# Attention of a two-layer block: batch 0 projected in two groups of four tiles, with the loads of K and Q between them

## The reference

```
q, k, v = xn @ Wq.T + bq, xn @ Wk.T + bk, xn @ Wv.T + bv
li, lj  = xn @ rel_W[:, :d].T, xn @ rel_W[:, d:].T
probs   = softmax(li[:, :, None, :] + lj[:, None, :, :] + rel_b, -1)     # three ways
bias    = einsum('bijk,hk->bhij', probs, logical_bias)
gate    = sigmoid(xn @ gate_W.T + gate_b)
weights = softmax(q k^T / 4 + gate * bias, -1)
x       = x + (weights @ v) @ Wo.T + bo
```

## Time and profile before

| | us |
|---|---|
| median of 3 runs | 6366.53 (6357.88 to 6370.67) |
| profiled execution, span | 6366.2 |
| first weight instruction of DVE | 26.96 |
| first score matmul of PE | 208.43 |
| first score row of DVE | 211.97 |
| last output store of the attention issued | 3194.31 |

### The profile page before, as it was taken

One profiled execution on the slowest core, in us unless ns is written; L12 is line 12 of the kernel. 1 busy time (PEld: TensorE's weight loads), 2 busy tenths in 40 slices (PEclk: granted clock), 3 DMA queues, 4 the chain that ended last, 5 costly groups with the idle time before them and its releaser, 6 DMA issues. The chain is left out here.

```text
span 6366.2 us, 126141 instructions
## 1 busy us (share of the span) xinstructions
PE 5502.0 (86%) x40354; PEld 3579.2 (56%) x40354; DVE 4670.8 (73%) x6108; ACT 4439.8 (70%) x7115; POOL 3699.2 (58%) x2063
## 2 busy tenths in 40 slices
PE   3688888888888888888879977999999979999999
PEld 3466666666666666665534434555555546666665
DVE  1688988888888888888878958999999961221221
ACT  1698998989899898999936668888888851111111
POOL 2677777777777777777610008999999960000000
PEclk7899999999999999999989989999999999999999
DMA  1212111121211212120035556555555541111110
GB/s 34 43 27 46 29 37 35 27 47 26 47 27 28 45 26 48 28 45 18 13 120 189 213 187 217 204 186 206 189 199 202 206 164 34 33 33 49 33 33 10
DMA packets 470082, 538.37 MB, mean 85 GB/s; under 512 B 251056, under 2 KB 345008, under 8 KB 469568
## 3 DMA queue, kind: packets, MB, share of 16 engines
q1 hardware_dynamic: 469568, 531.63, 27.3%
HBM read 370.18 MB, written 161.35 MB: 83 GB/s over the span
## 5 line engine op out<-in xcount | busy, mean ns | idle before, releaser
L317 DVE CUSTOM_DVE_ANT_0 srow<-srow,ps_s,cur 128x1024 f32<-128x1024 f32 x1024 | 1304.0, 1273 | 262.9 <-PE ps_s L465 180.8
L394 ACT ACTIVATE srow<-srow,nmax 128x1024 f32<-128x1024 f32 x1024 | 1190.9, 1163 | 207.6 <-DVE nmax L317 195.0
L403 ACT COPY AT<-ps_t 128x512 f32<-128x512 f32 x2048 | 1104.9, 597 | 74.8 <-PE ps_t L476 74.0
L476 PEld LDWEIGHTS ps_t<-ident,srow 128*128 128x128 f32 x8192 | 962.7, 143 | 279.1 <-ACT AT L403 84.1
L476 PE MATMUL ps_t<-ident,srow 128*128 128x128 f32 x8192 | 1105.0, 279 | 13.1 <-ACT AT L403 8.7
L1725 POOL TENSOR_TENSOR c_hc<-c_hs,c_cs 128x1024 f32<-128x1024 f32 x432 | 1009.8, 2363 | 60.8 <-DVE c_hs L1827 58.9
L465 PE MATMUL ps_s<-K,Q 96*128 96x512 bf16 x2048 | 632.3, 391 | 440.3 <-DVE nmax L317 318.5
L306 DVE SCALAR_TENSOR_TENSOR srow<-ps_p,rho,R 128x1024 f32<-128x1024 f32 x768 | 975.4, 1270 | 13.7 <-ACT ps_p L357 9.2
L1686 PE MATMUL c_ps_y<-c_hc,c_ident 128*128 128x512 f32 x2048 | 944.8, 594 | 30.0 <-POOL c_hc L1725 17.1
L1827 DVE TENSOR_TENSOR_SCAN c_hs<-c_da,c_pd 128x1024 f32<-128x1024 f32 x384 | 860.2, 2274 | 54.6 <-PE c_pd L1677 54.0
L1770 ACT ACTIVATE c_sT<-c_dxT,c_bT 128x256 f32<-128x256 f32 x1536 | 668.4, 494 | 106.8 <-PE c_pd L1677 96.6
(11 more groups left out here) (196 smaller groups left out, 8361.8 us busy)
## 6 DMA issues: line engine op xcount, KB each, us to landing
c_cs<-bc_d SPq DMA_DIRECT2D x256, 512.0 KB, 4.3
c_bs<-bc_d SPq DMA_DIRECT2D x64, 512.0 KB, 6.7
parts_d<-parts SPq DMA_DIRECT2D x65, 384.0 KB, 3.3
K<-parts_d SPq DMA_DIRECT2D x192, 128.0 KB, 4.6
Q<-parts_d SPq DMA_DIRECT2D x384, 64.0 KB, 2.9
sz_d<-b_sz SPq DMA_DIRECT2D x16, 1024.0 KB, 7.1
xv_d<-b_xv SPq DMA_DIRECT2D x16, 1024.0 KB, 7.7
dt_d<-b_ab SPq DMA_DIRECT2D x16, 1024.0 KB, 4.2
```

Of the source, the lines that this page charges most:

```text
L317: nc.vector.tensor_tensor_reduce(r[:], r[:], ps_s[:], cur[k][:, h:h + 1], BIG, ALU.add, ALU.min, nmax[:, h % NROW:h % NROW + 1]).then_inc( ...
L394: nc.scalar.activation(r[:], r[:], ACT.Exp, scale=-1.0, bias=nmax[:, h % NROW:h % NROW + 1]).then_inc(e_ok, 1)
L403: nc.scalar.copy(AT[h % NAT][:, HG * half:HG * half + HG, :], ps_t[:, half]).then_inc(at_ok, 1)
L476: last = nc.tensor.transpose(ps_t[:, half, i, :], rows_sb[h % NROW][:, j * P:(j + 1) * P], ident[:])
```

## The change

- SP no longer loads `b_gT` and `lbT`. DVE makes them from the row of biases with a mask (a reduction of the identity) and three more reductions. The waits for weights now ask for six DMAs.
- The `project` loop is gone. The eight tiles of batch 0 are two groups `g` of four: one x load of 512 KB, statistics and normalisation of four tiles, eight transposes into `ps_t`, matmuls with 512 columns where there were 128 (`pe_g_d`, `pe_g_g`, `pe_g_q`, `pe_g_k`) into `ps_p`, `ps_s`, `ps_t`, V in pairs of tiles through `ps_s` (`pe_g_v`). DVE takes the remainder and the low part, which POOL took. Buffers of the loop that are still unused hold the group's data.
- Parts are stored by four DMAs of 384 KB a group. Behind group 0's, SP loads Q6 of tile 0 and the first 512 tokens of K6 (24 DMAs of 64 KB without waits, `g_k6`), behind group 1's the other 512 tokens, by head groups with the waits of before.
- Tile 0's three-way softmax has all its POOL passes on DVE, in between group 1's.
- Tile 8 is projected in between: turned and D and gate behind group 0's, Q and K behind group 1's V.
- The semaphores that the loop counts get their start values by increments; the next stage clears all of the attention's semaphores on SP.
- The loop over tiles, its order and its instructions are the same.

The diff, cut to the lists and to one helper of each kind:

```diff
+        def sp_first_keys(sp, half):
+            cut = slice(4 * P * half, 4 * P * half + 4 * P)
+            for g in range(HG):
+                if half:
+                    alone(sp, k6_in, 96 * g, sp_own)
+                for s, part in enumerate(K_PART):
+                    sp.dma_start(K6[HD * s:HD * s + HD, HG * g:HG * g + HG, cut],
...
+        def dve_g_rem(dve, g, s):
+            dve.wait_ge(g_hi, 2 * g + s + 1)
+            nc.vector.tensor_tensor(GQK[g][s], GQK[g][s], GPARTS[:, 2 * g + s, 0], ALU.subtract).then_inc(g_rem, 1)
+        def pe_g_rows(dst, w, g, m):
+            for c in range(DC):
+                last = nc.tensor.matmul(dst, w[:, c], GXT[g][:, c, :], start=(c == 0), stop=(c == DC - 1))
...
             def start(sp):
-                sp_keys(sp, 0)
+                for s in range(2):
+                    sp_g_parts(sp, 0, s)
+                alone(sp, g_st, 64, sp_own)
                 sp_q6(sp, 0, 0)
+                sp_first_keys(sp, 0)
+                for s in range(2):
+                    sp_g_parts(sp, 1, s)
+                alone(sp, g_st, 128, sp_own)
+                sp_first_keys(sp, 1)
                 sp_parts(sp, NT)
...
             def start(pool):
-                front(pool, NT)
-                pool_rel(pool, 0, 0, 0)
...
+                pool_g_rstd(pool, 0)
+                pool_rstd(pool, NT)
+                pool_g_rstd(pool, 1)
+                pool_gT(pool, NT)
+                pool_rem(pool, NT)
+                pool_lo(pool, NT)
                 pool_f(pool, 0, 0, 1)
...
             def start(dve):
+                dve_g_qk(dve, 0)
+                for s in range(2):
+                    dve_g_rem(dve, 0, s)
+                for s in range(2):
+                    dve_g_lo(dve, 0, s)
+                for j in range(2):
+                    dve_g_v(dve, 0, j)
+                dve_g_gate(dve, 0)
+                dve.wait_ge(g_dc, 2)
                 for step in range(2):
                     dve_rel(dve, 0, 0, step)
+                for n in range(2):
+                    first_rel(dve, n)
+                dve_g_qk(dve, 1)
+                dve_g_rem(dve, 1, 0)
+                first_sum(dve, 0)
+                dve_g_rem(dve, 1, 1)
+                first_sum(dve, 1)
+                for s in range(2):
+                    dve_g_lo(dve, 1, s)
+                for j in range(2):
+                    dve_g_v(dve, 1, j)
+                first_t(dve)
                 dve_y(dve, 0)
+                first_p(dve, 1)
+                first_p(dve, 0)
+                dve_qk(dve, NT)
+                dve_g_gate(dve, 1)
                 dve_f(dve, 0, 0, 0)
...
+            def start(pe):
+                pe_g_t(pe, 0)
+                pe_xT(pe, NT, 0)
+                pe.wait_ge(w_ready, 1)
+                pe_g_d(pe, 0)
+                pe_g_g(pe, 0)
+                pe_d(pe, NT, 0)
                 pe_g(pe)
+                pe.wait_ge(w_ready, 2)
+                pe_g_q(pe, 0)
+                pe_g_k(pe, 0)
+                pe_g_t(pe, 1)
+                for j in range(2):
+                    pe_g_v(pe, 0, j)
+                pe_g_d(pe, 1)
+                pe_g_g(pe, 1)
+                pe_g_q(pe, 1)
+                pe_g_k(pe, 1)
+                for j in range(2):
+                    pe_g_v(pe, 1, j)
                 for half in range(2):
+                    pe_qk_proj(pe, NT, 0, half)
+                pe.wait_ge(g_k6, 16 * 24)
...
                 pe_s(pe, 0, 0, 0)
...
+            for used in HELD["done"]:
+                sp.sem_clear(used)
```

More of the change, by code:

```diff
@@ new lines, in act_g_t, with act_g_d, act_g_e @@
+        def act_g_t(act, g):
+            act.wait_ge(g_t, g + 1)
+            nc.scalar.copy(GXT[g], ps_t[:].rearrange("p c i t -> p c (i t)")).then_inc(g_tc, 1)
+        def act_g_d(act, g):
+            act.wait_ge(g_d, g + 1)
+            nc.scalar.copy(Dj[:, :, 4 * P * g:4 * P * g + 4 * P], wide(ps_p)).then_inc(g_dc, 1)
+        def act_g_e(act, g):
+            act.wait_ge(g_g, g + 1)
+            for m in range(DC):
+                last = nc.scalar.activation(GE[g][:, m, :], ps_s[:, 4 * P * m:4 * P * m + 4 * P], ACT.Exp, scale=-1.0,
+                                            bias=b_gT[:, m:m + 1])
+            last.then_inc(g_ec, 1)
@@ new lines, in pe_g_t @@
+        def pe_g_t(pe, g):
+            pe.wait_ge(g_xn, g + 1)
+            if g:
+                pe.wait_ge(g_qc, g)
+            for c in range(DC):
+                for i in range(4):
+                    last = nc.tensor.transpose(ps_t[:, c, i, :], GXN[g][:, i, c * P:(c + 1) * P], ident[:])
+            last.then_inc(g_t, 1)
+        def pe_g_rows(dst, w, g, m):
+            for c in range(DC):
+                last = nc.tensor.matmul(dst, w[:, c], GXT[g][:, c, :], start=(c == 0), stop=(c == DC - 1))
+            return last
@@ new lines, in pe_g_d, with pe_g_g @@
+        def pe_g_d(pe, g):
+            pe.wait_ge(g_tc, g + 1)
+            if g:
+                pe.wait_ge(g_kc, g)
+            for i in range(2):
+                last = pe_g_rows(ps_p[:, 4 * P * i:4 * P * i + 4 * P], w_dj[:, :, i, :], g, i)
+            last.then_inc(g_d, 1)
+        def pe_g_g(pe, g):
+            if g:
+                pe.wait_ge(g_vc, 2 * g)
+            for m in range(DC):
+                last = pe_g_rows(ps_s[:, 4 * P * m:4 * P * m + 4 * P], w_gr[:, :, m * P:(m + 1) * P], g, m)
+            last.then_inc(g_g, 1)
@@ new lines, in pe_g_q, with pe_g_k, pe_g_v @@
+        def pe_g_q(pe, g):
+            for m in range(DC):
+                last = pe_g_rows(ps_t[:, m].rearrange("p i t -> p (i t)"), w_qk[:, :, m * P:(m + 1) * P], g, m)
+            last.then_inc(g_q, 1)
+        def pe_g_k(pe, g):
+            pe.wait_ge(g_dc, g + 1)
+            for m in range(DC):
+                last = pe_g_rows(ps_p[:, 4 * P * m:4 * P * m + 4 * P], w_qk[:, :, D + m * P:D + (m + 1) * P], g, m)
+            last.then_inc(g_k, 1)
+        def pe_g_v(pe, g, j):
+            if j == 0:
+                pe.wait_ge(g_ec, g + 1)
+            else:
+                pe.wait_ge(g_vc, 2 * g + 1)
+            for i in range(2):
+                at = (2 * j + i) * P
+                for c in range(DC):
+                    last = nc.tensor.matmul(ps_s[:, 4 * P * i:4 * P * i + D + H + 2], GXT[g][:, c, at:at + P],
+                                            w_vg[:, c, 0:D + H + 2], start=(c == 0), stop=(c == DC - 1))
+            last.then_inc(g_v, 1)
@@ L559, in followed, with run @@
             return t > 0 and t <= (B - 1) * NT if isinstance(t, int) else pro
[L561 removed]
+        def run(eng, start, body, finish, ends=False):
             def pairs(first, start_i, par, b):
@@ L645, in _ @@
-            sp.sem_inc(parts_w, 16)
-            sp_x(sp, 0, 0)
-            run(sp, start, project, body, finish, ends=True)
+            sp.sem_inc(parts_w, 16 * NT + 16)
+            sp.sem_inc(x_in_s, 16 * NT)
+            for g in range(2):
+                sp.dma_start(GX[g], x_in[4 * P * g:4 * P * g + 4 * P, :].rearrange("(i p) d -> p i d", p=P)
+                             ).then_inc(g_in[g], 16)
+                loads = (((row[:], rows.partition_broadcast(P)), (ident[:], ident_in),
+                          (w_vg[:], wvg[:, 0:D + H + 6].rearrange("(c p) n -> p c n", p=P)), (b_qk[:], bqk)),
+                         ((w_qk[:], wqk.rearrange("(c p) n -> p c n", p=P)),
+                          (w_o[:], wvg[:, D + H + 6:].rearrange("(c p) n -> p c n", p=P))))[g]
+                for dst, src in loads:
+                    sp.dma_start(dst, src).then_inc(w_in, 16)
```

290 lines of the change are left out of this document (191 added, 99 removed).

## The result

The changed kernel takes 6224.6 us (median of 4 runs, 6220.4 to 6226.2) against 6366.5 for the kernel before on the same chip (6357.9 to 6370.7): ratio 0.9778, 95% interval 0.9766 to 0.9789, so 142 us less (134 to 149). The profiled execution has a span of 6218.6, 147.6 under that of before. In every run a time is 1.8 above its span, so this execution is the lowest of the four (6220.4, 4.2 under their median), and that of before would be 6368.0, 1.5 above its median: 5.7 of the 147.6 lie in which executions were profiled.

The account below looks back on a forecast made before the run. The start before the attention's first score row was taken to set the end: 125.8 us earlier, less 7.6 given back by tile 0, gives 118.2, so 6366.2 - 118.2 = 6248.0 us. The range was 6237 to 6276.

Parts of the forecast that it names:

- one to one: Start of attention: every later stage waits for the loop over tiles, so a shift of the loop shifts the end equally.
- signs of being wrong: First score row after 115, clock at 0.50 between 23 and 36, or loop not within 10 us of before.
- Rival C: Loop over tiles runs slower as its code moves; 1.85 us more per tile would eat 118; chance 0.02.
- Loads: Inputs of the start: 48 tiny loads go, x and weights land at 370 GB/s, ready at 9.3 instead of 27.0.
- PE and its clock: Projection groups of the start: full clock, with 1.8 to 2 us charged for a half-clock beginning after each pause.
- Rival A: PE stays at half clock through the groups: 27.4 us in all, layernorm at 130.1, time 6276; chance 0.12.
- The two chains: Last stretch before the first score row: SyncE's K lands at 82.6, VectorE ends at 86.2, last by 2.3 us.
- Given back by tile 0: Tile 0 of the loop: 7.6 us of the earlier start lost, mostly x of tile 9 behind K loads.
- Rival B: SyncE's queue sets the start, not VectorE, with slower landings: 108.2 us earlier than before, time 6258; chance 0.18.
- Clearing of semaphores: Next stage: SyncE clears the attention's 80 semaphores in 4 us, covered by later idling; costs 4 without that cover.
- Tile 0's softmax on VectorE: Beside group 1: its sums lie between other work and cost 1.24 us each, where GpSimd took 2.34.
- The rule on small transfers: K's loads halved to 64 KB: by the rule a half group costs 6.9 us like a whole one, time 6252.

Follow-up runs that it names:

- v1: Changed kernel with its start reordered (low parts ahead of softmax sums, x of tile 9 ahead of K6's second halves): 6222.8 us (0.9776).
- e4: Changed kernel with batch 0's keys loaded whole, all behind both groups' stores: 6240.1 us (0.9803).
- e7: Changed kernel with pads that put xt 32, K6 and Q6 64 bytes past a multiple of 256: 6234.5 us (0.9795).
- f1: Changed kernel with 64 unused bytes a partition in front of lbT: 6235.4 us (0.9796).
- f2: Changed kernel with 128 unused bytes a partition in front of lbT: 6237.6 us (0.9797).
- g1: Changed kernel with K6 alone 32 bytes past a multiple of 256 (32 bytes in front, 224 behind): 6238.8 us (0.9797).
- g2: Changed kernel with xt alone 32 bytes past a multiple of 256 (32 bytes in front, 224 behind): 6229.2 us (0.9782).
- e3: Changed kernel with tile 0's seven softmax passes back on GpSimd: 6223.1 us (0.9775).
- f0: Changed kernel as it is, timed a second time: 6224.8 us (0.9779).
- f3: Changed kernel with batch 0's keys loaded whole behind both groups' stores, but x of tile 9 issued ahead of them: 6229.6 us (0.9783).

## Why the prediction was wrong

**The step that failed** is the first: "the loop over tiles behind it keeps its bodies", so that a shift of the loop is a shift of the end "one to one". The bodies stayed, the addresses that their DMAs write to did not. That is worth 17 us (10 to 24) by the run with nothing but the pad. 122.5 + 17 = 139.5 of the 142 measured; what is left is within the error. With the loop's addresses held, "one to one" does hold: the changed kernel off the multiples of 256 has a ratio of 0.9804 to the kernel before, and on them, with both kernels there, 0.9778 / 0.9973 = 0.9805. Either is some 124.5 us, for a start 122.5 us shorter. With 32 bytes more the changed kernel takes 6240.3, inside the forecast's own range (6238 to 6258). Of its own signs of being wrong the prediction named the right one: from the first score row to the last store the loop took 2982.3 us before and 2958.3 after, 24.1 less where 10 were allowed. Rival C looked for a loop that changes, but only for its code, and only for a loss. The diff held the sizes of `lbT` and `mask`, and the page of the Trainium skill cited for small transfers ("DMA: Bandwidth & Descriptors") holds the 256-byte rule; I priced neither.

The forecast of the start itself, 118.2 for 122.5, is in part luck: the first score row came 2.5 later than forecast and tile 0 gave back 6.8 less, two errors of opposite sign.

The start, by the prediction's steps:

| step | forecast | trace |
|---|---|---|
| weights there | 9.3 | 11.33 |
| tile 8 normalised | 18.3 | 19.95 |
| group 0's V done | 49.4 | 49.98 |
| group 1's low parts | 71.3 | 71.85 |
| K6 landed, first score matmul | 82.6 | 81.70 |
| first score row | 86.2 | 88.67 |
| first layernorm | 102.7 | 98.33 |

- *Loads*: 2.0 late. From 5.2 to 6.5 us the transfers fell to 164 and 225 GB/s; I had taken 370 throughout. By these figures that dip is worth about 0.6 us (an estimate); the rest isn't traced to one cause.
- *PE and its clock*: right in the time. Granted clock was 1.00 from 20 to 36, and half (0.50, 1.2 GHz) only after pauses. The slow beginning that I had put down to the clock came, 1.5 us for the 1.8 charged (the first eight matmul rows took 5.14 us, the eight from 30.68 on 3.60), but the granted clock reads 1.00 over them, so its cause isn't shown. Stretches 24:36, 49:52 and 72:78 of the windows view, in the columns of the earlier trace rows:

```profile
24.00:36.00 12.00, 12.00 (x41) 6.32 (x40) 2.71 (x5) 3.42 (x7) 1.07 (x1) 1.00 0.00 0
...
49.00:52.00 3.00, 3.00 (x6) 1.27 (x5) 1.85 (x6) 0.26 (x1) 0.00 (x0) 0.69 0.07 19
...
72.00:78.00 6.00, 5.39 (x16) 4.44 (x17) 1.82 (x5) 0.00 (x0) 0.00 (x0) 0.50 0.75 249
```

  Rival A falls (by its own terms it would have cost 2 x 13.9 - 1.8 = 26.0, and not 27.4). Both second pairs of V came at half clock with a wait of 4.18, as charged (3.8).
- *The two chains*: VectorE was last, as forecast, but by 6.0 us (88.67 - 82.71) and not 2.3. K6's half groups took 4.2 us each (16.84 / 4) where I had 5.7, and VectorE was 2.5 late: 0.5 at the second pair of V, and 2.0 in the gate, where two small instructions took six times as long beside GpSimd. The gate of group 0, without GpSimd beside it, had 0.20 for the first of them (and 0.17 for the copy):

```profile
50.30 0.20 DVE L280 TENSOR_SCALAR xr<-xr 128x64 f32<-128x64 f32 x1 [0.32 <-ACT xr L313]
...
84.10 1.15 POOL L374 TENSOR_TENSOR qkf<-qkf,parts 128x512 f32<-128x512 f32 x1 [50.95 <-ACT parts L547]
84.11 1.20 DVE L280 TENSOR_SCALAR attn<-attn 128x64 f32<-128x64 f32 x1 [0.94 <-ACT attn L313]
...
86.08 1.15 POOL L378 TENSOR_TENSOR parts<-qkf,parts 128x512 bf16<-128x512 f32 x1 [0.83 <-ACT parts L551]
86.13 1.12 DVE L286 COPY small<-attn 128x8 f32<-128x8 f32 x1
```

  Each ends with the GpSimd instruction beside it (85.31 and 85.25, 87.25 and 87.23). In v1 the first starts 0.22 behind GpSimd's and takes 0.98, again up to its end.

- *Given back by tile 0*: 7.6 forecast, 0.8 measured (123.3 - 122.5). The mechanism (x of tile 9 behind K6 in SyncE's queue) was right, as e4 shows with its wait of 10.95; its size was off, since three half groups took 12.6 and not 17.1, and x landed in 3.1 us, not in 5.0: just in time, for in five of the other traces (e7, f1, f2, g1, g2) VectorE waits 0.2 to 1.4 for it there. Rival B had the opposite sign of this error and falls.
- *Clearing of semaphores*: hidden. The next stage's first load comes 2.14 us behind the last store, as before (2.08), and b_xt is issued 7.97 behind it (7.87 before); the span keeps all of the attention's 147.4.
- *Tile 0's softmax on VectorE*: priced at 1.24 a pass, hidden between group 1's work. Right, and e3 adds that it wasn't needed.
- *The rule on small transfers* (the Trainium skill, "DMA: Bandwidth & Descriptors", "Rules for kernel authors"): the half groups cost 4.2 and not the 6.9 of whole ones, so the price worked out from it was wrong. The direction holds: a whole group takes 6.5 in the changed kernel (26.14 / 4), so half the bytes cost 64% of it.

## What to carry to other kernels

Before calling a part of a kernel unchanged, compare the addresses of what its DMAs touch: one small tensor allocated ahead moves them all. Put tensors that DMAs write while others stand behind them in the queue at multiples of 256 bytes (here only K6's place was clearly worth something) and pad explicitly so that a later edit can't undo it. When a block of loads is moved or split, look first at what stands behind it in the queue, not at its own readers.

## What the runs showed of the hardware

- A load into SBUF whose rows (256 bytes) begin off a multiple of 256 lands later: 64 KB in 2.9 us in place of 2.2 at 32, 128 or 224 bytes off, 2.6 to 2.7 at 64. For 128 KB in rows of 2 KB it is 4.4 to 4.6 in place of 4.3 to 4.4, so the traces touch; for the 128 KB of xt in rows of 1 KB (3.3 to 3.9) no difference shows.
- A store of 384 KB from rows of 256 bytes lands in 2.8 to 2.9 us from a multiple of 256, in 3.3 to 3.4 from 32, 128, 160, 192 or 224 past one.
- A VectorE instruction of 0.17 to 0.20 us took 1.12 and 1.20 where a GpSimd one of 1.15 started just ahead of it, and ended with it.
- Two traces of the changed kernel (the first and f0's) differ by 7.6 us in the loop, with medians that differ by 0.2. The 25 us of one pair of traces are 17 and such differences.
- Open: the exact address rule between 64 and 256, what K6's place costs beside the wait for x, whether Q6's and xt's places cost anything of their own, whether the loop's code placement is worth anything below 5 us, and the 4.8 us of f3.
